# The slot mixer in four groups of two units, three groups in flight, instead of two rounds of four units

## The reference

```python
h = gelu(concat([x, slot_mean]) @ w1 + b1)
route_logits = (h @ w2 + b2) / (abs(tau) + 0.1)
alpha = softmax over the 8 largest of 64 logits, 0 elsewhere
slot_input = einsum('bts,btd->bsd', alpha, x)
si = slot_input / (alpha.sum(axis=1) + 1e-08)
gi, gh = si @ Wih.T + bih, S @ Whh.T + bhh
r, z = sigmoid(i_r + h_r), sigmoid(i_z + h_z)
n = tanh(i_n + r * h_n)
S_new = (1.0 - z) * n + z * S
q, k, v = S_new @ wq + bq, S_new @ wk + bk, S_new @ wv + bv
attn = softmax(q k^T * DQ**-0.5)
y = layernorm(S_new + attn v) * ln_g + ln_b
slot_values = y @ wvp + bvp
out = einsum('bts,bsd->btd', alpha, slot_values) @ wo + bo
```

## Time and profile before

| | us |
|---|---|
| median of 3 runs | 1642.88 (1641.58 to 1644.1) |
| the profiled execution | 1643.71 |
| its span, first to last instruction | 1641.5 |
| slot mixer, first `hidden` product to last `residual` | 1512.5 to 1637.7 |
| rest of the span after it (last store) | 3.8 |

### The profile page before, as it was taken

The page is one execution under the profiler, slowest core; times in us unless marked ns, Lnnn a source line. Parts: engine busy times, 40 slices in busy tenths (PEclk is TensorE's granted clock), DMA queues, the critical chain, the costliest instruction groups (busy, mean ns, idle before and its releaser), DMA issues.

```text
span 1641.5 us, 30315 instructions
## 1 busy us (share of the span) xinstructions
PE 1502.2 (92%) x9070; PEld 1093.7 (67%) x9070; DVE 899.0 (55%) x2901; ACT 609.0 (37%) x1705; POOL 291.1 (18%) x409
## 2 busy tenths in 40 slices
PE   5999999859999979999999989979999999888886
PEld 2666666659999946777777667748777644565664
DVE  4788787632232225545555435656666455555755
ACT  3655555412233224444444423223444001443422
POOL 4555566330000040000000000110000011121000
PEclk9999999859999999999999989989999799998888
DMA  5111115249999830000000000010110100341000
GB/s 137 31 33 37 36 35 184 85 152 316 323 320 328 293 104 19 19 9 18 18 18 18 0 1 13 20 45 28 36 29 17 33 20 25 91 164 43 1 21 20
DMA packets 89654, 128.85 MB, mean 78 GB/s; under 512 B 17362, under 2 KB 74786, under 8 KB 84450
## 3 DMA queue, kind: packets, MB, share of 16 engines
q1 hardware_dynamic: 85954, 123.50, 23.5%
q0 software_dynamic: 2432, 4.34, 0.9%
q10 hardware_dynamic: 1184, 0.01, 0.0%
HBM read 112.87 MB, written 11.67 MB: 76 GB/s over the span
## 4 chain that ended last, share of the span: by engine, by line
PE 75%; DVE 8%; issue 8%; POOL 3%; ACT 3%; DMA 2%; SPq 0%; POOLq 0%; DVEq 0%; ACTq 0%
PE bank L2353 10%; PE bank L2501 9%; PE bank L2710 8%; PE bank L2361 6%; PE bank L2803 6%; PE bank L2469 5%; PE bank L2520 4%; PE bank L2480 4%; PE bank L2724 4%; PE bank L2756 3%; PE bank L2772 3%; PE bank L2442 2%; PE bank L2956 2%; PE bank L2403 1%; DMA work<-in_F_b1c 1%
## 5 line engine op out<-in xcount | busy, mean ns | idle before, releaser
L1620 DVE COPY work<-bank 128x300 f32<-128x300 f32 (+1 forms) x272 | 124.1, 490 | 143.4 <-PE bank L2480 142.1
L2501 PE MATMUL bank<-work 128*100 128x64 f32 (+1 forms) x1760 | 191.4, 260 | 10.4 <-DVE work L1620 8.6
L2501 PEld LDWEIGHTS bank<-work 128*100 128x100 f32 x1760 | 177.1, 171 | 35.4 <-issue 19.0
L1112 ACT ACTIVATE work<-bank,work 100x361 f32<-100x361 f32 (+1 forms) x272 | 158.9, 590 | 53.2 <-DVE work L1611 37.6
L1955 DVE SCALAR_TENSOR_TENSOR work<-bank,work 128x128 f32<-128x128 f32 x160 | 56.1, 351 | 160.4 <-PE bank L2710 148.4
L2710 PE MATMUL bank<-work 128*128 128x128 f32 x1216 | 142.8, 275 | 0.6 <-DMA work<-in_F_b1c 0.6
L2710 PEld LDWEIGHTS bank<-work 128*128 128x128 f32 x1216 | 140.6, 192 | 2.2 <-ACT work L1233 1.2
L1611 DVE TENSOR_REDUCE work<-bank 100x1 f32<-100x361 f32 x208 | 102.0, 529 | 67.0 <-PE bank L2469 64.5
L2480 PEld LDWEIGHTS bank<-ident,work 100*128 100x128 f32 x880 | 90.6, 143 | 43.7 <-issue 22.5
L2480 PE MATMUL bank<-ident,work 100*128 100x100 f32 x880 | 106.0, 254 | 8.5 <-ACT work L1112 8.1
L1233 ACT ACTIVATE work<-bank,work 128x128 f32<-128x128 f32 x160 | 58.8, 368 | 144.0 <-PE bank L2710 138.9
(11 more groups left out here) (343 smaller groups left out, 2767.0 us busy)
## 6 DMA issues: line engine op xcount, KB each, us to landing
work<-in_F_w SPq DMA_DIRECT2D x58, 1024.0 KB, 5.8
work<-in_ctxT SPq DMA_DIRECT2D x64, 180.5 KB, 2.4
work<-context_norms SPq DMA_DIRECT2D x32, 288.0 KB, 3.4
context_norms<-work SPq DMA_DIRECT2D x16, 288.0 KB
work<-in_ctx SPq DMA_DIRECT2D x16, 192.0 KB, 2.8
work<-in_F_b SPq DMA_DIRECT2D x20, 128.0 KB, 6.8
work<-sorted_x SPq DMA_DIRECT2D x20, 128.0 KB, 3.0
sorted_y<-work SPq DMA_DIRECT2D x20, 128.0 KB, 6.2
```

Source lines behind the costliest of these rows:

```text
L1112: nc.scalar.activation(pr[:, 0:NK], S_bank[k][0:T, 0:NK], ACT.Exp, bias=nmax[k][0:T, :], accum_out=rsum[j][0:T, h:h + 1]).then_inc(s.exped ...
L1620: nc.vector.tensor_copy(PT[k][:, 0:CH, :], PT_bank[k][:, 0:CH * T].rearrange("p (c t) -> p c t", c=CH)).then_inc(s.probs_copied.sem, 1)
L2501: ins = nc.tensor.matmul(to, PT[k][:, c, :], values, start=(c == 0), stop=(c == CH - 1))
```

## The change

The eight units go in four groups of two. In period p (0 to 3) group p does its early stages, group p - 1 its cell and group p - 2 its late stages, and each engine's program is written with the three mixed. After period 3, group 2 ("third" in the code) and group 3 ("last") do what is left of them, their late stages in turn.

Banks: the early stages use banks 0 to 3 (`2 * (k % 2)`), the late stages banks 4 to 7 (`late_bank`), those of the last group banks 0 to 3. `sums` of a group waits for the `rz_in` of the group before, and `s_turn` of groups 1 and 2 waits for the `residual` of the group before. `gru_in` becomes `gates_in` (512 columns) and `new_in` (256 columns). The turned alpha gets a buffer for each unit (`ALT`). The buffers of pair[2] and pair[3] lie where the weights of layer 2 were (F_weight in the order's names). The work on the weights moves into periods 0 and 1, `pick(2)` to the end of period 0 and `pick(3)` into period 1. In the opening, the mean's product stands ahead of `hidden(1)`.

The core of the diff:

```diff
-SLOT_ROUNDS = B // (2 * SLOTS_AT_ONCE)
+SLOT_GROUPS = B // 4
+LAST_GROUP = 2 * (SLOT_GROUPS - 1)
+def late_bank(u):
+    return (4 if u < LAST_GROUP else 0) + 2 * (u % 2)
...
                 hidden(0)
-                hidden(1)
                 begin(pe, 7)
                 slots_mean()
+                hidden(1)
                 hidden(2)
...
                 def sums(u, k):
-                    if u >= SLOTS_AT_ONCE:
-                        pe.wait_ge(s.resid, 2 * (u - SLOTS_AT_ONCE + 1))
+                    if u >= 2:
+                        pe.wait_ge(s.rz_in, 2 * (u - 1))
...
                 def s_turn(u, k):
                     pe.wait_ge(s.slots_new, 3 * (u + 1))
+                    if 2 <= u < LAST_GROUP:
+                        pe.wait_ge(s.resid, 2 * (u - 1))
...
-                for i in range(SLOT_ROUNDS):
-                    for k in range(SLOTS_AT_ONCE):
-                        sums(SLOTS_AT_ONCE * i + k, k)
-                        alpha_turn(SLOTS_AT_ONCE * i + k, k)
-                    each(i, gru_in)
...
-                    each(i, attn_turn, comm, y_turn, values, mixed)
+                for p in range(SLOT_GROUPS):
+                    late, early = p - 2, p
+                    both(s_turn, late)
+                    one(sums, early, 0)
+                    one(alpha_turn, early, 0)
+                    if p == 1:
+                        weights_product()
+                    both(qkv, late)
+                    one(attn, late, 0)
+                    one(sums, early, 1)
+                    one(alpha_turn, early, 1)
+                    one(attn, late, 1)
+                    one(gates_in, early, 0)
+                    both(attn_turn, late)
+                    one(new_in, early, 0)
+                    if p == 1:
+                        weights_mean()
+                    both(comm, late)
+                    one(gates_in, early, 1)
+                    both(y_turn, late)
+                    one(new_in, early, 1)
+                    if p == 0:
+                        weights_turn()
+                    both(values, late)
+                    both(mixed, late)
```

More of the change, by code:

```diff
@@ new lines, in slot_mixer @@
+                both(weights, 1)
+                for p in range(SLOT_GROUPS):
+                    late, cell, early = p - 2, p - 1, p
+                    both(slots_copy, late)
+                    one(rz_tanh, cell, 0)
+                    one(pooled, early, 0)
+                    if p == 1:
+                        weights_scaled()
+                    one(rz_tanh, cell, 1)
+                    one(qk_copy, late, 0)
+                    one(n_tanh, cell, 0)
+                    one(pooled, early, 1)
+                    one(qk_copy, late, 1)
+                    one(n_tanh, cell, 1)
+                    both(attn_exp, late)
+                    if p == 0:
+                        weights_copy()
+                    else:
+                        both(weights, early + 1)
+                    both(y_copy, late)
@@ new lines, in slot_mixer @@
+                third, last = SLOT_GROUPS - 2, SLOT_GROUPS - 1
+                one(rz_tanh, last, 0)
+                both(slots_copy, third)
+                one(rz_tanh, last, 1)
+                one(n_tanh, last, 0)
+                one(qk_copy, third, 0)
+                one(n_tanh, last, 1)
+                one(qk_copy, third, 1)
+                both(slots_copy, last)
+                both(attn_exp, third)
+                both(qk_copy, last)
+                both(y_copy, third)
+                both(attn_exp, last)
@@ L1391, in slot_mixer @@
+                both(y_copy, last)
                 end(act)
@@ L2240, in slot_mixer @@
                 biased(0)
                 pick(0)
[L2242 to L2245 removed]
+                for n in range(1, B // 4):
+                    biased(n)
+                both(alpha, 0)
                 pick(1)
[L2247 to L2254 removed]
+                both(alpha, 1)
@@ new lines, in slot_mixer @@
+                gru_fixed()
+                for p in range(SLOT_GROUPS):
+                    late, cell, early = p - 2, p - 1, p
+                    one(rz_in, cell, 0)
+                    if p == 1:
+                        pick(3)
+                    one(rz_in, cell, 1)
+                    one(v_done, late, 0)
+                    one(alpha_copy, early, 0)
+                    one(rz_done, cell, 0)
+                    one(v_done, late, 1)
+                    one(masked, late, 0)
+                    one(rz_done, cell, 1)
+                    one(masked, late, 1)
+                    one(alpha_copy, early, 1)
+                    one(slots_new, cell, 0)
+                    both(attn_copy, late)
+                    one(slots_new, cell, 1)
+                    both(y_stats, late)
+                    if p == 0:
@@ L2255, in slot_mixer @@
                         pick(2)
-                        pick(3)
-                    each(i, v_done, masked)
-                    if i == 0:
+                    if p == 1:
                         weights_centered()
-                    each(i, attn_copy, y_stats, values_done)
-                    if i + 1 < SLOT_ROUNDS:
-                        each(i + 1, alpha)
-                    each(i, residual)
+                    if p > 0:
+                        both(alpha, early + 1)
+                    both(values_done, late)
@@ new lines, in slot_mixer @@
+                    both(residual, late)
+                third, last = SLOT_GROUPS - 2, SLOT_GROUPS - 1
+                both(rz_in, last)
+                both(rz_done, last)
+                one(slots_new, last, 0)
+                one(v_done, third, 0)
+                one(slots_new, last, 1)
+                one(v_done, third, 1)
+                both(masked, third)
+                both(attn_copy, third)
+                one(v_done, last, 0)
+                both(y_stats, third)
+                one(v_done, last, 1)
@@ L2264, in slot_mixer @@
+                both(masked, last)
+                both(values_done, third)
+                both(attn_copy, last)
+                both(residual, third)
+                both(y_stats, last)
+                both(values_done, last)
+                both(residual, last)
                 end(dve)
@@ new lines, in slot_mixer @@
+                third, last = SLOT_GROUPS - 2, SLOT_GROUPS - 1
+                both(s_turn, third)
+                both(qkv, third)
+                one(attn, third, 0)
+                both(s_turn, last)
+                one(attn, third, 1)
+                one(qkv, last, 0)
+                both(attn_turn, third)
+                one(qkv, last, 1)
+                both(comm, third)
+                one(attn, last, 0)
+                both(y_turn, third)
+                one(attn, last, 1)
+                both(values, third)
@@ L3055, in slot_mixer @@
+                both(attn_turn, last)
+                both(mixed, third)
+                both(comm, last)
+                both(y_turn, last)
+                both(values, last)
+                both(mixed, last)
                 end(pe)
```

226 lines of the change are left out of this document (95 added, 131 removed).

## The result

The changed kernel takes 1624.89 us (median of 6 runs, 1620.29 to 1632.21) against 1642.08 us for the one before (6 runs, 1640.38 to 1644.1): ratio 0.9896, 95% interval 0.987 to 0.9922. The profiled execution took 1626.69 us with a span of 1624.8, 17.0 us less than the one of before.

What follows compares the result with a forecast made beforehand. TensorE was taken to bound the mixer, through idle waits, half clock and work. The walk's 22.8 us gain, less 7.0 and 1.8, gave 14.0 us: 1642.9 to 1628.9 us, range 1620 to 1637.

Steps and rivals of the forecast that it cites:

- The opening: Before the first sums: moving the mean's product ahead of hidden(1) gains 0 us (bounds -1 and +0.3).
- Period 0: First group's early stages: gates start at 1529.75 instead of 1534.84; the 1.2 us wait and clock fall stay.
- Period 1: TensorE needs 11.7 us with no wait over 0.3; the sums of period 2 start at 1550.55.
- Hand-over: Between periods: residuals after the last mixed (1.2 us), then rz_in (1.06 us), before the next sums can run.
- Periods 2 and 3: Each period takes 19.9 us: 17.6 from first sums to last mixed, plus 1.2 and 1.06.
- 16.95 us of work: TensorE's work in periods 2 and 3 from the first sums: 17.5 us less 0.55 for the transposes ahead.
- The end: After period 3: qkv of unit 4 starts 3.4 us after mixed; last residual at 1614.9, 22.8 us earlier than before.
- The clock: Half-clock loss in the mixer behind the first fall: 7.0 us taken off the walk's 22.8 us gain.
- 1.8 us of hand-offs: The second amount taken off the walk's 22.8 us gain, 1.8 us.
- the signs that I had named: Profile signs, including sums behind about 1.7 us ended by rz_in, 2 to 3.5 us before unit 4's qkv; wrong: pooled over 1 us.
- the clock holds: Rival: no clock fall after the first in the mixer, 21 us less, 1622 us; chance 0.13.
- The queues couple: Rival: late results hold all chained groups, ten places at 0.7 us cost 7 us, 1636 us; chance 0.18.

Runs made afterwards that it cites:

- the hand-over alone: Changed kernel with the next cell's first rz_in ahead of the late residuals, the next sums ahead of the s_turns, rz_tanh ahead of slots_copy: 1624.54 us, ratio 0.9885.
- all together: Changed kernel with the hand-over reordered, qk_copy ahead of pooled, and three extra 256-column products ahead of the last y_turns: 1622.68 and 1619.69 us on two chips.
- the last one: The "all together" kernel plus alpha_copy ahead of gru_fixed, three extra products before the first gates, and pick(3) moved to period 2: 1623.68 us, ratio 0.9876.

## Why the prediction was right

Predicted 1628.9, range 1620 to 1637; measured 1624.9, and the forecast mechanism is what the profile shows. Step by step:

- *The opening:* 0, as booked: from the first `hidden` product to the first sums 13.1 us in both kernels.
- *Period 0:* the start of the gates held to 0.1 us, 4.23 us after the first sums (walk 4.18), half clock until about 1533.6. That dense products instead of two more units' sums pay was shown by the kernel with gru_in early: 6.5 us by itself. I had booked this only as a start 5 us sooner; it also shortens the same fall in the second round, from 10.2 us to 3.4.
- *Period 1:* the sums of period 2 come 24.5 us after the first sums (walk 25.0).
- *Hand-over:* 2.25 us (walk 2.3), and the chain residual, rz_in, sums was shown by taking it apart: 0.46 us from the last mixed to the sums there.
- *Periods 2 and 3:* 20.9 us instead of 19.9. The term "16.95 us of work" was too small: from the first sums to the last mixed it is 18.7 us and not 17.6. The wait of 0.5 us for qk_copy is there; TensorE is busy for 18.2 us instead of 16.95. I put the difference down to the drain where stages of a few products alternate, which I had left out as "without the drain at each group's end"; no run tests this alone. 1.1 us each.
- *The end:* the wait for slots_copy is there as walked (3.2 us to qkv; walk 3.4). From qkv to the end it takes 27.5 us instead of 23.4, of which two falls of the clock are 3.3 (24.2 us where the clock held).
- *The clock:* the mis-sized term. I added 7.0 us behind the first fall; the profiled execution lost 3.3, and the second and third profiles of the same kernel lost 6.3 (1.6 of it at the first gates) and 4.7. The clock held at the hand-over in the first and fell there in the other two. So the term is a spread, 3 to 7, and not a constant.

The sum in the end: walk 22.8, less the 3.3 of the clock and 2.2 of the rest, is 17.3 us, the difference of the two profiles. The rest is 2.1 us more in the two periods and 0.7 at the end, less 0.5 in period 1 and 0.2 at the wait for slots_copy; I had booked 1.8 us of hand-offs for it. Against the same profile of before the mixers of the other two executions are 14.3 and 15.9 us shorter, so where between 14 and 17 the difference falls is in part luck with the clock.

Of the signs that I had named, three did not come as written. The sums of period 3 stood behind 0.64 us ended by rz_in and not 1.7, because 0.8 us of the hand-over are waits of the s_turns for the residuals, ahead of them; the wait on ScalarE's copy before the qkv of unit 4 was 1.6 us and not 2 to 3.5; and the gates waited 1.4 us for `pooled`, which I had called a sign of being wrong although the walk itself kept a wait of 1.2 us there. The list was at odds with the walk; the walk was right.

Of the rivals, "the clock holds" (1622) did not come true: the clock fell somewhere behind the first gates in all three profiles, at half the price that I had booked in the first. "The queues couple" is out: no period was above 21 us where the clock held; the 22.4 us of one period in the third profile are a fall of the clock in it. A rival that I had not listed has a share: some 6 us come from the order of sums and gru_in alone, which needs neither groups of two nor the offset.

Open: how far the versions behind the change are better. By the stretches at full clock the order is worth 1.1 us for the hand-over alone, 2 us for all together and 3 us for the last one, but medians of 4 to 6 executions that spread over 4 to 10 us do not show it, and much of that spread arises ahead of the mixer. Open too is a part of the gain: on the other two chips the medians fell by 20 us, 4 to 6 us more than the mixers there are shorter than the one profile of before, and no profile of the kernel before was taken on those chips.

## What to carry to other kernels

When all units of a round wait at the same stage, put groups at an offset, and walk each in-order queue at the hand-over: what must be finished there before the first instruction of the next group can run is the price of a period, here residual, rz_in, bank. Groups made smaller without the offset make it worse. Before pipelining, look at what runs right behind a wait: here long products first kept the half clock to 3.4 or 6.8 us, four units' sums first to 10.2. Where the clock falls at other places in each execution, hold an edit against several profiles of the unedited kernel, stretch by stretch: a fall that is gone from one profile is no effect yet. And split a wait so that each product waits only for its own input.

## What the runs showed of the hardware

The granted clock fell behind stretches of short products with waits of only 0.5 us (period 2 of the kernel with extra products, and of the unedited changed kernel in its third profile), and at one and the same hand-over it held in one execution and fell in two others. In the kernel before it stayed at 0.50 for 10.2 us, twice, where four units' sums (64 columns) ran first. With gates of 512 columns first it stayed there for 3.4 us in the change's first profile and in the kernel with gru_in early and the split wait (in both rounds), for 6.8 us in the change's second profile and in the kernel with gru_in early alone (in both rounds), and it did not fall at all at the first gates in the third.
